# Transformer layer on one core: the maxima of the first two head groups computed beside the last three projected batches, and the order of the first loads and last stores

## The reference

```python
qkv = einsum('bsd,ndh->bnsh', x, W_qkv); q, k, v = split(qkv, 3)
attn = softmax(einsum('bnqh,bnkh->bnqk', q, k) * 0.25 + causal_mask)
out = einsum('bnqk,bnkh->bnqh', attn, v).reshape(B, -1, S)
a = einsum('bds,nhd->bsd', out, W_out)      # n and h summed: rows of W_out are added up
x1 = layernorm(x + a)
xm = mix over neighbouring tokens of x1     # then x1 + picked path, twice normed
```

## Time and profile before

| | us |
|---|---|
| median of 3 runs | 1630.11 (1629.15 to 1633.2) |
| the profiled execution's own time | 1630.98 |
| its span, first to last instruction | 1629.0 |
| PE busy in the span | 1497.6 (92%) |
| DVE busy | 1099.3 (67%) |
| ACT busy | 953.6 (59%) |
| POOL busy | 446.8 (27%) |
| DMA queue q1, share of 16 engines | 42.4% |

### The profile page before, as it was taken

The page is one execution under the profiler, slowest core; times in us unless marked ns, Lnnn a source line. Parts: engine busy times, 40 slices in busy tenths (PEclk is TensorE's granted clock), DMA queues, the critical chain, the costliest instruction groups (busy, mean ns, idle before and its releaser), DMA issues. The chain is left out here.

```text
span 1629.0 us, 30478 instructions
## 1 busy us (share of the span) xinstructions
PE 1497.6 (92%) x9050; PEld 726.0 (45%) x9050; DVE 1099.3 (67%) x1749; ACT 953.6 (59%) x2103; POOL 446.8 (27%) x563
## 2 busy tenths in 40 slices
PE   5979988999998998998998998999998999999995
PEld 3546533343343343343333333433423566656664
DVE  3212258778776776776776776777752688878875
ACT  3536521767666766766766666676676455545442
POOL 5424310111123213212213313313324262222222
PEclk9989976999999999999999999999999999999998
DMA  4887771123363373382382373374371532101001
GB/s 133 265 279 250 262 228 29 58 58 114 99 113 87 96 148 85 96 160 76 99 160 72 109 156 69 94 167 79 91 115 50 112 75 92 45 21 52 26 27 39
DMA packets 166778, 178.57 MB, mean 110 GB/s; under 512 B 26397, under 2 KB 135784, under 8 KB 166632
## 3 DMA queue, kind: packets, MB, share of 16 engines
q1 hardware_dynamic: 166632, 176.70, 42.4%
HBM read 109.79 MB, written 66.06 MB: 108 GB/s over the span
## 5 line engine op out<-in xcount | busy, mean ns | idle before, releaser
L784 DVE TENSOR_REDUCE a_mx<-a_ps_m 128x1 f32<-128x640 f32 (+6 forms) x704 | 700.0, 1027 | 234.2 <-PE a_ps_m L857 233.5
L764 ACT ACTIVATE a_probs<-a_ps_s 128x512 f32<-128x512 f32 (+3 forms) x1536 | 641.2, 498 | 307.5 <-PE a_ps_s L911 300.5
L852 PE MATMUL a_ps_m<-s_ks,s_qs 96*128 96x512 bf16 (+3 forms) x1536 | 396.9, 343 | 38.2 <-DVE a_mx L784 24.7
L911 PE MATMUL a_ps_s<-s_qs,s_ks 99*128 99x512 bf16 (+3 forms) x1536 | 388.7, 332 | 27.0 <-issue 16.9
L719 POOL TENSOR_SCALAR_AFFINE_SELECT a_probs<-a_probs 128x512 f32<-128x512 f32 x256 | 163.2, 637 | 733.9 <-ACT a_probs L764 733.9
L887 PE MATMUL a_ps_o<-a_probs,s_vq 128*32 128x512 f32 (+3 forms) x3072 | 329.6, 501 | 0.7 <-POOL a_probs L719 0.7
L852 PEld LDWEIGHTS a_ps_m<-s_ks,s_qs 96*128 96x128 bf16 x1536 | 127.5, 100 | 295.9 <-DVE a_mx L784 143.2
L911 PEld LDWEIGHTS a_ps_s<-s_qs,s_ks 99*128 99x128 bf16 x1536 | 127.8, 98 | 193.8 <-ACT a_probs L764 102.0
L857 PE MATMUL a_ps_m<-s_mask,s_ident 128*128 128x128 bf16 (+2 forms) x864 | 206.2, 239 | 0.0
L1395 PE MATMUL f_ps_o<-f_w,f_hm 128*128 128x256 f32 (+1 forms) x640 | 152.4, 386 | 0.9 <-DVE f_y L1302 0.9
L226 DVE TENSOR_TENSOR p_rest<-p_ps_qk,h_space 128x512 f32<-128x512 f32 x64 | 44.2, 691 | 154.8 <-ACT h_space L251 154.8
(11 more groups left out here) (120 smaller groups left out, 1132.9 us busy)
## 6 DMA issues: line engine op xcount, KB each, us to landing
qk_parts<-h_space SPq DMA_DIRECT2D x64, 384.0 KB, 2.9
s_qs<-qk_parts SPq DMA_DIRECT2D x192, 128.0 KB, 2.8
s_ks<-qk_parts SPq DMA_DIRECT2D x192, 128.0 KB, 2.8
v_rows<-h_space SPq DMA_DIRECT2D x16, 896.0 KB, 5.4
s_vq<-v_rows SPq DMA_DIRECT2D x32, 448.0 KB, 4.0
f_x_in<-in_L_attn_x_dram SPq DMA_DIRECT2D x16, 512.0 KB, 6.2
heads_out<-a_o_sb SPq DMA_DIRECT2D x128, 64.0 KB
f_x_in<-in_L_attn_x_dram SPq DMA_DIRECT2D x8, 1024.0 KB, 8.6
```

The costliest lines, as they stand in the source:

```text
L764: act.activation(probs[:, st % PB, h, 0:width], ps_s[:, n % BANKS, 0:width], ACT.Exp, scale=SCALE).then_inc(exps[h % 2], 1)
L784: dve.tensor_reduce(mx[:, e, heads[0]:heads[-1] + 1, qt], span(i), AX_X, ALU.max)\
L852: last = pe.matmul(out, qs[0:TROWS, j, h, q], ks[0:TROWS, j, h, s:s + wide], start=k == 0, stop=mask is None)
L911: pe.matmul(ps_s[:, n % BANKS, 0:width], ks[0:MROWS, j, h, kt * P:(kt + 1) * P], qs[0:MROWS, j, h, q0:q0 + width], start=True, stop=True)\
```

## The change

- `Maxima` is a class of its own; its tiles and semaphores live through both stages. In the projection it has one unit buffer (`ps_m`, two banks); `ps_t` and `ps_v` shrink to one bank each (`ps_t` by halves k, `ps_v` by halves r), which makes ScalarE copy x in two halves.
- In batches 5, 6 and 7 (AHEAD = 5), now written out, each chunk takes STEPS_IN = 8 units (the last chunk 4) between its transposes T, products P and values V. The loops before attention's first slot are gone, and W_out's sums move to the start of batch 5.
- x of batch b + 1 is loaded from ScalarE's queue, after the copy of the second half. The first x chunk is issued ahead of the projection weights, the 23 weight DMAs right behind the second.
- The weights are packed half by VectorE, half by ScalarE. The ones in `ks` are written by VectorE after the chunks of batch 0 instead of by GpSimd at the start.
- Quads 0, 1 and 2 are loaded in pieces of 3 to 5 DMAs after the stores of a chunk, quad 3 at the start of attention. The waits for the last stores stand behind that load.
- `head.constants` (GpSimd) moves from the start of attention to its last batch.

The core of the diff (`Maxima` holds the former functions `banks`, `span`, `rows`, `take_max`, `turn_max`, `split_max` and `send_max`, unchanged in what they compute):

```diff
+UNITS = [((h,), qt) for qt in range(CT, TILES) for h in range(QUAD)]
+UNITS += [(tuple(range(h, h + 2)), qt) for qt in (3, 2) for h in range(0, QUAD, 2)]
+UNITS += [(tuple(range(QUAD)), 1)]
+TURN = 2
+UNITS.insert(TURN, (tuple(range(QUAD)), 0))
+NU = len(UNITS)
...
+AHEAD = 5
+STEPS_IN = 8
...
+        ps_t = pb("p_ps_t", [P, CHUNK], F32)
         ps_qk = pb("p_ps_qk", [P, QKM, CHUNK], F32)
+        ps_v = pb("p_ps_v", [P, 2, D], F32)
+        ps_m = pb("p_ps_m", [P, RBANKS, CHUNK], F32)
...
+        def ahead(b, c, s):
+
+            k = (CHUNKS * (b - AHEAD) + c) * STEPS_IN + s if isinstance(b, int) else -1
+            return divmod(k, NU) if 0 <= k < 2 * NU else None
...
             @block.sync
...
+                PLAN = {(2, 0): (0, 0, 3), (2, 1): (0, 3, 6), (3, 0): (0, 6, 9), (3, 1): (0, 9, 13),
+                        (4, 0): (1, 0, 3), (4, 1): (1, 3, 6), (5, 0): (1, 6, 9), (5, 1): (1, 9, 13),
+                        (6, 1): (2, 0, 4), (7, 0): (2, 4, 8), (7, 1): (2, 8, 13)}
...
+                        if (b, c) == (BATCH - 1, CHUNKS - 1):
+                            load_piece(sp, quads, qk_parts, v_rows, 0, *PLAN[b, c])
                         store(b, c)
+                        if (b, c) in PLAN and (b, c) != (BATCH - 1, CHUNKS - 1):
+                            load_piece(sp, quads, qk_parts, v_rows, 0, *PLAN[b, c])
+                        if (b, c) == (6, 1):
+                            maxima.send(sp, 0, 0)
+
+                load_x(sp, 0, 0)
+                for c in range(KC):
+                    sp.dma_start(w[:, c, :, :], w_qkv[:, c * P:(c + 1) * P, :].rearrange("n p e -> p n e"))\
+                        .then_inc(w_loaded, 16)
+                load_x(sp, 0, 1)
+                load_weights(sp)
...
             @block.vector
...
                 for qk in range(2):
+                    pack(dve.tensor_copy, qk, 0).then_inc(w_packed[0], 1)
...
+                        unit(0)
+                        unit(1)
+                        remain(0)
+                        unit(2)
+                        remain(1)
+                        unit(3)
+                        unit(4)
+                        unit(5)
+                        remain(2)
+                        unit(6)
+                        unit(7)
+                        remain(3)
+                        if isinstance(b, int) and b == 0:
+                            for j in range(2 * c, 2 * c + 2):
+                                dve.memset(ks[TROWS:P, j, :, :], 1.0)
+                        if isinstance(b, int) and (b, c) == (AHEAD, 0):
+                            dve.wait_ge(wsum_cut, 2)
...
             @block.scalar
...
+                def keep_x(b, c, k):
+                    act.wait_ge(xt_made, KC * (b * CHUNKS + c) + k + 1)
+                    act.activation(x_t[:, c, k, :], ps_t[:, :], ACT.Copy).then_inc(xt_kept, 1)
+                    if k == KC - 1 and not (isinstance(b, int) and b == BATCH - 1):
+                        load_x(act, b + 1, c)
...
+                        if ahead_of:
+                            keep_x(*ahead_of, 0)
+                        if not isinstance(u, int) or u:
+                            middle(u - 1, 1 - c, QKM - 1)
 
                         act.wait_ge(parts_stored[c], 16 * QKM * b)
+                        high(u, c, 0)
+                        high(u, c, 1)
+                        middle(u, c, 0)
+                        if ahead_of:
+                            keep_x(*ahead_of, 1)
+                        else:
+                            high(u, c, 2)
+                        middle(u, c, 1)
+                        if ahead_of:
+                            act.wait_ge(v_stored[c], 16 * b)
+                            keep_v(u, c, 0)
+                            high(u, c, 2)
+                            keep_v(u, c, 1)
+                            middle(u, c, 2)
+                            high(u, c, 3)
...
             @block.tensor
...
+                def rows(v, i):
+                    if not v and not i:
+                        pe.wait_ge(loaded[0], LOADS)
+                        pe.wait_ge(wsum_kept, 1)
+                    else:
+                        pe.wait_ge(maxima.rows_max, NU * v + i)
...
+                        def values(r):
+                            if not isinstance(u, int) or u or r:
+                                pe.wait_ge(v_kept, 2 * u + r)
...
+                        if ahead_of:
+                            transposes(*ahead_of, 0)
+                        unit(0)
+                        pe.wait_ge(xt_kept, KC * (u + 1))
+                        product(0)
+                        unit(1)
+                        product(1)
+                        unit(2)
+                        if ahead_of:
+                            transposes(*ahead_of, 1)
+                            unit(3)
+                            values(0)
+                            unit(4)
+                            product(2)
+                            unit(5)
+                            values(1)
+                            unit(6)
+                            product(3)
+                            unit(7)
+                        else:
+                            unit(3)
+                            product(2)
+                            product(3)
+                            values(0)
+                            values(1)
...
 def attend_stage(...)
...
-                for j in range(2, QUADS):
-                    load_quad(sp, quads, qk_parts, v_rows, 0, j)
-                load_weights(sp)
-                send_max(0, 0)
+                load_quad(sp, quads, qk_parts, v_rows, 0, QUADS - 1)
+                for c in range(CHUNKS):
+                    sp.wait_ge(stored[0][c], 16 * BATCH * 2 * HEADS * HD // P)
+                    sp.wait_ge(stored[1][c], 16 * BATCH)
...
-                for v in range(2):
-                    pe.wait_ge(loaded[v], LOADS)
-                    for i in range(NU):
-                        rows(v, v, i)
-                pe.wait_ge(w_loaded, WEIGHT_DMAS)
-                pe.wait_ge(sum_ones, 1)
```

More of the change, by code:

```diff
@@ L76, in project_stage, with load_piece @@
-def project_stage(nc, x, w_qkv, qk_parts, v_rows, space, x_in, consts, quads):
+def load_piece(sp, quads, qk_parts, v_rows, b, j, first, end):
+    qs, ks, vq, loaded = quads
+    for d in range(first, end):
+        if d == 2 * len(TERMS):
+            sp.dma_start(vblocks(vq)[:, j, :, :].rearrange("p t v -> p (t v)"), v_quads(v_rows, b)[j])\
+                .then_inc(loaded[j], 16)
+            return
+        i = d // 2
+        dst, r, part = ((qs, 0, TERMS[i][0]), (ks, HEADS * HD, TERMS[i][1]))[d % 2]
+        r += j * QUAD * HD
+        sp.dma_start(dst[i:TROWS:len(TERMS), j, :, :],
+                     qk_parts[b, r:r + QUAD * HD, part, :].rearrange("(n h) s -> h n s", h=HD))\
+            .then_inc(loaded[j], 16)
@@ L80, in project_stage @@
+def project_stage(nc, x, w_qkv, qk_parts, v_rows, residual, maxima, weights, stored, head, x_in,
+                  consts, quads):
     with ExitStack() as ctx:
@@ L90, in project_stage @@
         ident, ident16, mask16 = consts
-        ks, vq = quads[1], quads[2]
+        ks, vq, loaded = quads[1:]
+        wout, load_weights, weights_loaded = weights
+        parts_stored, v_stored = stored
+        space = head.space
+        ones = residual.aw_sb[:, 0, 0:P]
+        wide = residual.inv_in[:, :, 0, :]
         QKM = 2 * HEADS * HD // P
@@ L203, in _ @@
                 turn(0)
-                with pool.Fori(1, BATCH) as b:
+                with pool.Fori(1, AHEAD) as b:
+                    turn(b)
+                cut()
+                for b in range(AHEAD, BATCH):
                     turn(b)
@@ L221, in turn, with unit, remain @@
                         u = b * CHUNKS + c
-                        dve.wait_ge(lo_done, u * QKM)
-                        for m in range(QKM):
+                        def unit(s):
+                            if ahead(b, c, s):
+                                v, i = ahead(b, c, s)
+                                maxima.take(dve, ps_m[:, :, :], v, v, i)
+                                if v and i == TURN:
+                                    maxima.split(dve, ps_x, 0)
+                        def remain(m):
+                            if not isinstance(u, int) or u:
+                                dve.wait_ge(lo_done, (u - 1) * QKM + m + 1)
                             dve.wait_ge(hi_done, u * QKM + m + 1)
@@ L312, in _, with output_sums @@
+                def output_sums():
+                    pe.wait_ge(weights_loaded, WEIGHT_DMAS)
+                    pe.wait_ge(sum_ones, 1)
+                    WC = HEADS * HD // P
+                    for a in range(WC):
+                        last_mm = pe.matmul(ps_m[:, 0, 0:D], ones, wout[:, a, :], start=(a == 0), stop=(a == WC - 1))
+                    last_mm.then_inc(wsum_made, 1)
+                for k in range(KC):
+                    transposes(0, 0, k)
```

(12 more changed lines are left out.)

407 lines of the change are left out of this document (189 added, 218 removed).

## The result

| us | before | after |
|---|---|---|
| median of 4 runs each, on one chip | 1630.84 (1629.15 to 1633.2) | 1592.18 (1589.62 to 1595.22) |
| profiled execution, its span | 1630.98, 1629.0 | 1589.62, 1587.9 |
| first score of slot 0 | 274.07 | 243.06 |
| from there to the end of the span | 1354.9 | 1344.8 |
| mean granted clock | 0.961 | 0.982 |

The ratio is 0.9763, 95% interval 0.974 to 0.9786; a later measurement, with 5 runs after and 9 before, gave 1593.82 against 1629.69, 0.9783 (0.9767 to 0.9799). The forecast was 1599 with a range of 1581 to 1614. The range holds the result; the forecast's own range, 1594 to 1605, begins just above it.

What follows compares the result with a forecast made beforehand. PE was taken to bound the projection, VectorE's maxima the next stage's opening. The terms sum to a first score at 242.4 us, 31.7 earlier, carried unchanged to the end: 1599 us, 8-in-10 range 1581 to 1614, the forecast's own 1594 to 1605.

Steps and rivals of the forecast that it cites:

- first product: Projection start: with x and weights issued early and packing hidden, PE's first product comes at 11.0 us instead of 21.69.
- clock in the first chunk: Projection start: PE's clock is at half for its first microseconds, allowed 2.0 us instead of 1.0.
- fills on VectorE: Batch 0: two memsets per chunk delay ScalarE's copy of v; PE waits 5.0 us plus 1.8 of half clock, twice: 13.6.
- waits for DMA in them: Batches 0 to 4: busy DMA engines make PE wait 1 us, bounds 0 and 12.8.
- sums and unit 0: Once, at W_out's sums: four V instructions, the rest of a wait for ScalarE's copy, and unit 0: 1.6 us.
- five chunks with units: Batches 5 to 7: eight units a chunk, with waits at units 0 and 3, make it 16.95 us; five take 84.8.
- last chunk and split: End of the projection: last chunk with three units 13.9 us, and splitting slot 0's maxima 0.7.
- hand-over: Projection to attention: the last stores' landing is no longer waited for; 1.6 us plus 0.3 for the engines' meeting.
- Rival A: Batch 0: VectorE's fills are hidden, so the 13.6 us fall away, 1586 us; chance 0.22.
- Rival B: Projection: the DMA engines saturate and stores come late, with PE behind them; up to 12.8, say 10 us, 1609; chance 0.20.
- rival C: Batches 5 to 7: waits at units 0 and 3 pull the clock down, up to 85 us, about 1680; chance 0.04.
- D: Batches 5 to 7: units are not covered, each of eight waits its full 1.2 us; 40 us, 1639; chance 0.04.

Runs made afterwards that it cites:

- the two versions that hide them: Changed kernel with the fills of ones given to GpSimd, 1578.97 us; or kept on VectorE as eight halves, one behind each chunk of batches 0 to 3, 1579.18 us.
- the timed profile: The changed kernel without edits, profiled a third time and timed beside the kernel before: 1593.82 us, first score 243.3, 1349.1 us behind it.
- the last version: Changed kernel with the fills in halves over batches 0 to 3 and attention's batches written out on PE, ScalarE and VectorE: 1557.90 us, ratio to before 0.956.
- three engines written out without the halves: Changed kernel with attention's batches written out on PE, ScalarE and VectorE, fills left whole: 1574.92 us, ratio to before 0.9668.

## Why the prediction was right, and the step of it that failed

| term of the first score | forecast | profile |
|---|---|---|
| first product | 11.0 | 10.84 |
| clock in the first chunk | 2.0 | 2.6 (24.60 - 10.84 - 11.19) |
| fills on VectorE | 13.6 | 15.7 (62.64 - 24.60 - 2 x 11.19 = 15.66) |
| ten chunks | 111.9 | 111.9 |
| waits for DMA in them | 1.0 | 0 |
| sums and unit 0 | 1.6 | 1.5 |
| five chunks with units | 84.8 | 84.4 (226.91 - 142.51) |
| last chunk and split | 14.6 | 14.5 |
| hand-over | 1.9 | 1.7 |
| first score | 242.4 | 243.06 |

The ten chunks are put at 11.19 us each in both columns, so the 1.5 is what is left of 142.51 - 62.64 after seven of them.

*The fills.* The mechanism is right: the fills stand ahead of a remainder, ScalarE's order hangs on it, V's one bank waits for ScalarE, and PE waits twice (5.0 forecast; 5.23 and 5.30). That the wait is so close is luck in part, as two links were off and cancel. The rate was read from a row's length, 0.70 us for 768 elements, so 3.7 us a fill. The distance from one start to the next is what a fill holds the engine: in the same row 1.50 less 0.70, 0.80 us, which gives 4.3. The pair, with the idle time before it, took 8.65 us where the working has 7.4. Behind it ScalarE took 2.98 us (34.33 to 37.31) to come to V where the working has 3.95: the issue of x's load, costed at 0.67, ran beside an activation (both at 35.08). The term's size is off by the clock, of which I allowed 1.8 us a wait: the two chunks leave 3.2 and 1.9 (19.64 and 18.40 less 11.19 and the wait). In the first of them P behind V still took 3.08 us instead of 1.88. Rival A fell: the fills were not hidden, and the two versions that hide them lie 14.8 and 14.6 us below the change (1593.82), where it would have put a hidden fill.

The Trainium skill's cycle per element for a memset (VectorE: DVE Perf Modes, "Zero memsets can be issued as uint32 (trn2)") gives, at that page's 0.96 GHz, 4.27 us, an estimate. The trace agrees with it by the distance from one fill to the next, 4.27 us (26.59 to 30.86); the rows' own 3.47 us read short, and by such a row the prediction wrongly doubted the page. By the page the term would have been 15.8 us, near the 15.7, but with waits of 6.2 us where the rows show 5.3. The packing copies at 0.25 us each without GpSimd's memset agree with the rule of exclusion that the prediction took from the Trainium skill (SBUF — State Buffer, "Who interferes with whom"); VectorE's 3.87 us pair was waiting, not work.

*x.* The waits of the earlier trace rows went, for the reason given: x no longer stood in SyncE's order behind the stores and `load_quad`. Rival B had the DMA engines saturated at 0.98. They were at 0.97 from 84 to 136 us and no chunk was late, while x on SyncE gave waits at 0.76. In this kernel the share was no measure of lateness; the time at which the load was issued was.

*The units.* For a maximum PE waits at units 0 and 3 alone, 0.4 to 0.9 us where 0.76 was forecast; 1.3 at the most, in the last chunk. Beside them stand two waits that the prediction put at nothing, 0.6 us for quad 1 and 0.5 for the turning of slot 0's maxima. The clock at 1.00 ends rival C: bf16 units between float32 products don't bring it down. D did not occur.

*The step that failed* is the last: "the last instruction the same distance behind it as today", from "Behind it the same slots and the same feed-forward follow, so I carry its shift to the end"; a change of that distance was one of its own signs of being wrong. The distance fell by 10.1 us in the first profile, 4.1 and 5.8 in the other two (from 1354.9). It splits at the last score of slot 31. Attention, first to last score: 975.8 and 973.6 us before, 970.2 to 976.8 in the eight profiles of the changed kernel whose attention code is the same, with a mean of 974.0. So there is no difference there beyond the luck of the clock; the first profile had the lowest of the eight, with only one of its five returns followed by the longer of the two half-clock stretches (6.8 us instead of 3.4). The feed-forward: 379.1 and 379.7 before, 374.6 to 377.6 after with a mean of 376.3. The two sets don't overlap. Against the timed profile the difference is in one place: from the last score to VectorE's last row ahead of the return of the feed-forward's loop are 176.5 us before (1426.44) and 176.6 after (1393.15), so what differs comes behind it. (The other profiles vary by up to 2.7 us elsewhere too, with the clock.) VectorE at the return of the feed-forward's loop, before (first fence) and after (timed, second):

```profile
1429.86 0.43 DVE L1250 BATCH_NORM_STATS2 f_st_b<-f_y 128x6 f32<-128x256 f32 x1 [2.73 <-issue]
1431.89 1.08 DVE L1250 BATCH_NORM_STATS2 f_st_b<-f_y 128x6 f32<-128x256 f32 x3 [1.59 <-issue]
```
```profile
1396.63 1.40 DVE L1382 BATCH_NORM_STATS2 f_st_b<-f_y 128x6 f32<-128x256 f32 x4 [2.79 <-issue]
```

Before, VectorE stops a second time after the first of the four statistics, 1.59 us. PE meets it 15 us later, again before and after:

```profile
1446.36 0.39 PE L1453 MATMUL f_ps_h<-f_pick_t,f_widen 128*128 128x512 bf16 x1 [2.54 <-DVE f_hm L1297]
```
```profile
1411.44 0.39 PE L1585 MATMUL f_ps_h<-f_pick_t,f_widen 128*128 128x512 bf16 x1 [0.91 <-DVE f_hm L1429]
```

The wait is 1.6 us longer and a half-clock stretch of 3.4 us follows it, 1.7 more: 3.3 us. From PE's row to the end of the span are 182.7 and 181.0 us, which is that 1.7. The second stop is in both profiles of the kernel before (1.59 and 1.62) and in none of the twelve of versions of the changed one. The feed-forward's code is the same; what differs is the program ahead of it. In the last version, whose VectorE program ahead of it differs again, VectorE's return shows no stop at all, where three engines written out without the halves still has 2.8 us. That the loop's instructions lie elsewhere and are fetched otherwise is my reading, and only argued; no run moved that code alone.

So the forecast's 31.7 should have read 31.0 + 3.3 = 34.3. The medians say 38.7 (1630.84 - 1592.18; by the interval of the ratio 34.9 to 42.4) and 35.9 in the later measurement (1629.69 - 1593.82; 32.8 to 38.0). The sum lies inside the second and just under the first; what is over it isn't settled.

## What to carry to other kernels

Ask of each filler instruction how long it holds its engine in one piece, idle time before its row included, and what is queued behind it there: the fills cost 15 us where two stood in a row on VectorE, and nothing in halves of 2.3, or in a row on GpSimd, behind whose work PE doesn't stand. Give a load that must be on time a queue whose order holds nothing that waits; a busy share of the DMA engines of 0.97 did no harm, stores that wait for their parts ahead of the load did. Read a loop's return as work of every engine, some 3 us of PE and 2.5 of ScalarE here, with the half clock behind it, and write the loop out on the engine that bounds first, then on the one that shows up next.

## What the runs showed of the hardware

A loop's return left PE idle 2.9 to 3.8 us, five times, 15.7 to 16.9 us in all; ScalarE 2.4 to 2.7; VectorE 2.5 to 2.8, with a second stop in the loop's body that came and went with the program around it. No such stop is left on VectorE in the feed-forward of the last version (feed-forward 374.7 us), though that loop is still there. Behind each return of PE's attention loop the granted clock was at half for a stretch, 3.4 or 6.8 us long, and which of the two came differed between executions of the same kernel. In the changed kernel's projection it stayed at 1.00 behind waits of up to 1.3 us between float32 products. Longer ones went both ways: with x on SyncE a wait of 2.2 us was followed by a stretch at half (clock 0.79 from 96 to 104 us), one of 2.9 us was not (1.00 from 136 to 144 us). Memsets on VectorE held it longer than their rows say: 4096 elements 3.47 us in the row and 4.27 from start to start; GpSimd takes 3.51 to 3.54 us in the row for the same fill and 3.57 to 3.60 from start to start (both in the kernel before).
